# Second cross attention: where the row sums are taken, how the maximum is negated, where the scale is applied

## The reference, cut to what matters

```python
def _L1_xattn_ref(queries, keys, values, Wq, Wk, Wv, Wo):
    q = (queries @ Wq).reshape(b, s, KV_HEADS, GROUP, HEAD_DIM)      # 8 x 4 x 16
    k = (keys @ Wk).reshape(b, s, KV_HEADS, HEAD_DIM)
    v = (values @ Wv).reshape(b, s, KV_HEADS, HEAD_DIM)
    scores = jnp.einsum('bqhgd,bkhd->bhgqk', q, k) * (1.0 / sqrt(HEAD_DIM))
    attn = jax.nn.softmax(scores, axis=-1)
    out = jnp.einsum('bhgqk,bkhd->bqhgd', attn, v)
    return out.reshape(b, s, EMBED) @ Wo
```

## Time and profile before

| | us |
|---|---|
| median of 3 runs | 2617.96 (2616.93 to 2624.43) |
| the profiled execution | 2622.04, of which the span from first to last instruction is 2620.3 |
| the stage of the change, 64 steps | 2367.6 to 2567.0 of the span, 199.4 |
| one pair of batch rows in its middle (i = 1, m = 5 to i = 2, m = 4) | 2435.2 to 2486.3, 51.1 |
| TensorE busy over the span | 94% |

### The profile page before, as it was taken

The page is one execution under the profiler, slowest core; times in us unless marked ns, Lnnn a source line. Parts: engine busy times, 40 slices in busy tenths (PEclk is TensorE's granted clock), DMA queues, the critical chain, the costliest instruction groups (busy, mean ns, idle before and its releaser), DMA issues.

```text
span 2620.3 us, 39586 instructions
## 1 busy us (share of the span) xinstructions
PE 2468.7 (94%) x13387; PEld 2095.4 (80%) x13387; DVE 1306.9 (50%) x2988; ACT 932.6 (36%) x2492; POOL 744.5 (28%) x440
## 2 busy tenths in 40 slices
PE   5999899999999999977899999999999999868997
PEld 3788788888888888856688888888888888756665
DVE  6445444444444444464444444444444444476674
ACT  2111344444444444421233333333333333216672
POOL 4245432222222232211311211211211111136670
PEclk9999899999999999988899999999999999978998
DMA  3110221112111111101111111111111111010000
GB/s 110 57 48 24 89 81 48 64 48 76 52 64 48 62 66 48 66 6 43 41 43 42 42 42 42 42 42 46 56 50 51 42 42 42 10 47 1 1 0 33
DMA packets 37552, 121.59 MB, mean 46 GB/s; under 512 B 4984, under 2 KB 7416, under 8 KB 37504
## 3 DMA queue, kind: packets, MB, share of 16 engines
q1 hardware_dynamic: 37504, 120.97, 13.3%
HBM read 118.86 MB, written 2.10 MB: 46 GB/s over the span
## 4 chain that ended last, share of the span: by engine, by line
PE 86%; DVE 7%; issue 3%; POOL 3%; ACT 2%; SPq 0%; DMA 0%; POOLq 0%; DVEq 0%; ACTq 0%
PE pj L502 18%; PE pj L503 18%; PE pj L504 18%; PE ou L502 7%; PE ou L504 6%; PE ou L503 6%; PE pv L742 2%; PE sc L633 2%; PE sc L733 2%; PE pv L649 2%; DVE probs L1163 2%; PE tp L640 1%; PE tp L819 1%; POOL probs L485 1%; POOL w_lo L386 1%
## 5 line engine op out<-in xcount | busy, mean ns | idle before, releaser
L378 POOL TENSOR_TENSOR w_lo<-raw,w_hi 128x1024 fp32r<-128x1024 f32 x144 | 344.0, 2389 | 1443.8 <-ACT w_hi L905 1443.8
L502 PE MATMUL pj<-xt_hi,w_hi 128*128 128x512 f32 (+2 forms) x1296 | 519.3, 401 | 9.4 <-DVE act_lo L1120 3.8
L503 PE MATMUL pj<-xt_lo,w_hi 128*128 128x512 f32 (+2 forms) x1296 | 502.5, 388 | 0.0
L504 PE MATMUL pj<-xt_hi,w_lo 128*128 128x512 f32 (+2 forms) x1296 | 501.8, 387 | 0.0
L502 PE MATMUL ou<-w_hi,act_hi 128*128 128x512 f32 x684 | 276.5, 404 | 17.2 <-DVE act_lo L1439 6.9
L502 PEld LDWEIGHTS pj<-xt_hi,w_hi 128*128 128x128 f32 x1296 | 246.8, 190 | 55.7 <-issue 5.6
L504 PEld LDWEIGHTS pj<-xt_hi,w_lo 128*128 128x128 f32 x1296 | 245.7, 190 | 49.9
L503 PEld LDWEIGHTS pj<-xt_lo,w_hi 128*128 128x128 f32 x1296 | 246.9, 190 | 41.7
L1126 DVE TENSOR_TENSOR x<-x,ou 128x512 f32<-128x512 f32 (+1 forms) x200 | 136.3, 685 | 284.6 <-PE ou L504 284.6
L504 PE MATMUL ou<-w_hi,act_lo 128*128 128x512 f32 x684 | 269.2, 394 | 0.0
L503 PE MATMUL ou<-w_lo,act_hi 128*128 128x512 f32 x684 | 268.6, 393 | 0.0
(11 more groups left out here) (246 smaller groups left out, 4918.4 us busy)
## 6 DMA issues: line engine op xcount, KB each, us to landing
raw<-in_l1a_w SPq DMA_DIRECT2D x80, 512.0 KB, 3.6
raw<-in_l0x_w SPq DMA_DIRECT2D x64, 512.0 KB, 3.8
side<-in_side SPq DMA_DIRECT2D x32, 512.0 KB, 4.2
raw<-in_ffn_w SPq DMA_DIRECT2D x15, 512.0 KB, 3.3
side<-in_ctx_t SPq DMA_DIRECT2D x8, 512.0 KB, 3.3
raw<-in_l1x_w SPq DMA_DIRECT2D x7, 512.0 KB, 4.0
raw<-in_l0f_w SPq DMA_DIRECT2D x6, 512.0 KB, 4.1
raw<-in_taylor_w SPq DMA_DIRECT2D x5, 512.0 KB, 7.1
```

What stands on the lines that cost most here:

```text
L378: pool.tensor_tensor(WL[:, s, :], RAW[:, s, :], f32(WH[:, s, :]), ALU.subtract).then_inc(w_ready[s], 1)
L502: pe.matmul(out, wh, xh, start=first, stop=False)
L503: pe.matmul(out, wh, xl, start=False, stop=False)
L504: return pe.matmul(out, wl, xh, start=False, stop=last)
```

## The change

Four edits, all in the second cross attention. The activation of the exponentials loses its scale and its `accum_out`. The scale 1/4 is applied where the queries leave PSUM: in ScalarE's copy and in VectorE's subtraction, which becomes a scalar_tensor_tensor. The maximum is written negated by the reduction itself, so the multiplication behind it and the wait between the two are gone. The row sums are taken by a VectorE reduction over the exponentials in SBUF (128 x 512 to 128 x 4), placed between `row_max(m + 1)` and the reciprocal, with a semaphore (`lx_sum`) between the sum and the reciprocal.

```diff
                 def queries(f):
                     fill = nth(PJ["l1x"], i, KC, f)
-                    hi(fill, q1(AH, f % KC), pj[fill[1]][:, 0:256])
+                    hi(fill, q1(AH, f % KC), pj[fill[1]][:, 0:256], HD ** -0.5)
 
                 def exps(m):
                     n, bank = nth(0, i, 16, m)
                     act.wait_ge(lx_nm, n + 1)
                     for h in range(GQ):
-                        at = bank * GQ + h
                         done = act.activation(PR[:, bank, h * S:(h + 1) * S], sc[bank][:, h * S:(h + 1) * S], ACT.Exp,
-                                              bias=NM[:, bank, h:h + 1], scale=HD ** -0.5,
-                                              accum_out=SUMS[:, at:at + 1])
+                                              bias=NM[:, bank, h:h + 1])
                     done.then_inc(lx_exp, 1)
...
                 def queries(f):
                     fill = nth(PJ["l1x"], i, KC, f)
-                    lo(fill, i * KC + (HI["l1x"] + f), q1(AL, f % KC), pj[fill[1]][:, 0:256], q1(AH, f % KC))
+                    lo(fill, i * KC + (HI["l1x"] + f), q1(AL, f % KC), pj[fill[1]][:, 0:256], q1(AH, f % KC), HD ** -0.5)
 
                 def row_max(m):
                     n, bank = nth(SC["l1x"], i, 16, m)
                     dve.wait_ge(sc_full, n + 1)
-                    dve.tensor_reduce(MX[:, bank, :], sc[bank][:].rearrange("p (h s) -> p h s", h=GQ),
-                                      axis=AX.X, op=ALU.max).then_inc(lx_max, 1)
-                    dve.wait_ge(lx_max, i * 16 + (m + 1))
-                    dve.tensor_scalar(NM[:, bank, :], MX[:, bank, :], -HD ** -0.5, None, ALU.mult).then_inc(lx_nm, 1)
+                    dve.tensor_reduce(NM[:, bank, :], sc[bank][:].rearrange("p (h s) -> p h s", h=GQ),
+                                      axis=AX.X, op=ALU.max, negate=True).then_inc(lx_nm, 1)
 
                 def row_recip(m):
                     dve.wait_ge(lx_exp, i * 16 + (m + 3))
                     at = slice(m % 2 * GQ, (m % 2 + 1) * GQ)
+                    dve.tensor_reduce(SUMS[:, at], PR[:, m % 2, :].rearrange("p (h s) -> p h s", h=GQ),
+                                      axis=AX.X, op=ALU.add).then_inc(lx_sum, 1)
+                    dve.wait_ge(lx_sum, i * 16 + (m + 1))
                     dve.reciprocal(RC[:, at], SUMS[:, at]).then_inc(lx_rc, 1)
```

More of the change, by code:

```diff
@@ L236, in build @@
         pads_zero, pad_ready, on_done, lx_pn = (sem(n) for n in ("pads_zero", "pad_ready", "on_done", "lx_pn"))
-        kr_full, kr_hi, kr_lo, kx_ready, lx_max, lx_nm, lx_exp, lx_rc, lx_on = (sem(n) for n in
-            ("kr_full", "kr_hi", "kr_lo", "kx_ready", "lx_max", "lx_nm", "lx_exp", "lx_rc", "lx_on"))
+        kr_full, kr_hi, kr_lo, kx_ready, lx_sum, lx_nm, lx_exp, lx_rc, lx_on = (sem(n) for n in
+            ("kr_full", "kr_hi", "kr_lo", "kx_ready", "lx_sum", "lx_nm", "lx_exp", "lx_rc", "lx_on"))
         dq, w_deq, bias_added = sem("dq"), sem("w_deq"), sem("bias_added")
```

## The result

The changed kernel takes 2633.98 us, median of 5 runs (2631.98 to 2635.57), against 2617.96 before; the ratio is 1.0059, 95% interval 1.0049 to 1.0070. It is slower by 16 us, 0.6%. The forecast was 2630. The profiled execution took 2632.96, 10.9 above the profiled one of before.

The account below looks back on a forecast made before the run. A two-step chain through VectorE and GpSimd was taken to bound the stage, no engine being full. Pair costs 3.4 + 2.9 + 2.9 + 2.7 = 11.9, say +12, on the 2618 median gave 2630 us, range 2619 to 2641.

Parts of the forecast that it names:

- The loop: Two-step chain: scores, VectorE maximum, reciprocal, GpSimd product, TensorE transposes; 4.66 us before, 5.12 forecast.
- maximum to product: From the start of VectorE's maximum to GpSimd's product: 1.21 us in an undelayed step before, 1.67 forecast.
- The walk through the middle pair: Accumulated lateness of each step's transposes, i = 1 step 5 to i = 2 step 4: 2.9 us per middle pair.
- step 5: First step counted, in i = 1: its transposes were to start 0.49 us later.
- The first pair: Stretch up to step 4 of the second pair, its first three steps hanging on TensorE: 3.4 us more.
- The last pair: Final stretch of the stage, from step 5 on: 2.7 us more.
- Quiet steps 2.5 to 2.6 apart: Steps hanging on VectorE and GpSimd, not behind a projection: transposes 2.56 us apart instead of 2.33.
- ScalarE's lighter load: Exponentials without accumulator reads: saving between 0 and 0.36 us a step, taken as 0 because ScalarE is off the critical chain.
- The held sum: Rival: VectorE's row sum is delayed while GpSimd works, some 45 steps paying 0.8 us; +36 us, 2654; chance 0.05.
- The faster case: Rival: the removed multiplication's delay under GpSimd work was the true cost; 6.5 us gained, 2611; chance 0.08.
- turning point of 0.39: Cost in us of the row sum on the path below which the change would turn into a gain.
- The neutral case by the count of instructions: Part of the no-measurable-change rival (chance 0.18): VectorE still has four instructions a step, so 2618.

Follow-up runs that it names:

- the narrow sum: Changed kernel with the row-sum reduction reading 128 x 32 ones instead of 128 x 512 exponentials, softmax not normalised by its sums: 2617.64 us, original 2620.70.
- one half of this one: Changed kernel with row sums back on ScalarE, leaving the scale in the queries and the negating maximum: 2614.82 us, ratio to the original 0.9977.
- sum only: Original kernel with just the row sums moved to VectorE, the multiplication and its wait kept: 2651.54 us, ratio to the original 1.0121.
- double sum: Changed kernel with the row-sum reduction done twice, first into a tile nobody reads: 2664.74 us, original 2619.11.

## Why the prediction was right

**Direction and size.** 2630 was forecast, 2634 came; +12 on the profiled execution was forecast, +10.9 came. That these two lie so close owes something to chance, since the profiled difference holds +1.2 us ahead of the first scores, most of it clock, and -1.1 in the first three steps, by the clock too, and these cancel; but the steps at full clock alone also give about 11.

**The loop.** Its links came out as written: maximum to product 1.68 (1.67 forecast), the sum 676 ns (between the bounds 553 and 687, taken as 0.69). The walk through the middle pair gave 0.49 for step 5 (measured 2.95 - 2.46 = 0.49), and 2.9 for the pair (measured 53.94 - 51.08 = 2.86, and 2.93 for the next). Between these two it also holds: counted from step 4, the transposes come later by 0.58, 0.67, 1.05, 1.22, 1.71 and 1.88 at steps 6, 8, 9, 11, 13 and 15 (forecast 0.63, 0.71, 1.10, 1.28, 1.76, 1.92), and by 2.38, 2.23 and 2.87 at steps 1 to 3 of the next pair (2.40, 2.27, 2.90). TensorE's wait for GpSimd was to grow from 13 to some 25 us; it is 27.1.

**Mis-sized terms.** The first pair was put at 3.4 us and came to 1.8 (37.09 + 26.27 against 37.12 + 24.49); 1.1 us of the missing 1.6 are the clock, which rose earlier in the profile after. The last pair was put at 2.7 and came to 2.3; its last step to pay, 13-14, paid only 0.17 (3.29 against 3.12). "Quiet steps 2.5 to 2.6 apart" was right only as a mean: they come as 2.42 and 2.71, since the loop of two steps splits unevenly. And ScalarE's lighter load, taken at 0, is worth 1.1 us in the later steps, most of it where VectorE waits for its copy of the queries.

**The rivals.** The held sum: no sum of 64 was over 686 ns, against the 1.03 of the multiplication. The Trainium skill, "GPSIMD Engine Reference", section "1. Specifications", puts the contention on VectorE instructions in a 2-port mode or with two SBUF inputs; the 64 sums, with one input, agree. The faster case: its gain is real (4.4 us in the steps, 5.9 in the total), but the sum takes it back more than three times. Its turning point of 0.39 for the sum lies between what the two widths showed: 0.18 gave less than before, 0.68 more. The neutral case by the count of instructions: the narrow sum kept the count at four and the wide one too, and they lie 11.5 us apart, so the count alone decides nothing here.

**What the prediction lacked** is a term for the clock. It speaks of the chain alone; the medians moved 3 to 5 us more than the chain, and that is why 2634 came and not 2630.

## What to carry to other kernels

Before work is moved from one engine to another, look at which of the two is on the loop, not at which is busier: here ScalarE was busier and its reads cost the steps at full clock 1 us, while the same sums on VectorE, busy 65% of the stage, cost 14, because they stand between a maximum and a product that TensorE waits for. Take a change with several parts apart: one half of this one is worth 6 us, the other costs more than twice that. A tiny instruction can be the dear one; compare its mean with its minimum (343 and 170 ns) before its width.

## What the runs showed of the hardware

- A VectorE multiplication from 128 x 4 to 128 x 4 in SBUF takes 0.17 us and up to 1.04 when GpSimd works. Reductions of 128 x 512 (687 ns on average from PSUM, 674 to 686 from SBUF), the reciprocal (178 to 181 in the kernel after) and the statistics (694 on average) beside the same work do not lengthen. The mean of the multiplication changed from 343 to 592 ns when its neighbours moved, with nothing changed in itself.
- Four exponentials of 128 x 128 without `accum_out` start 0.25 us apart and take 1.14 us, with it they start 0.34 apart, and the last read follows; that is 0.09 us saved for each, the upper bound of the prediction. A row of ScalarE in the kernel after:

```profile
2450.03 1.14 ACT L1071 ACTIVATE probs<-sc,neg_max 128x128 f32<-128x128 f32 x4
```

- The granted TensorE clock at the start of this stage is at the lower of its levels, 1.2 GHz. In the twelve profiles it rose between 2376.7 and 2402.3 us, and with that the total differs by some 10 us between executions and between kernels whose steps are nearly alike. In the two kernels with the longest waits of TensorE (sum only, double sum) it also fell in mid-stage, for 3 to 20 us at a time; that the waits are the reason is not shown.
